# A hybrid of attention, convolution and expert layers: moving set-up work of the first stages beside the first attention, and the output's turn beside the last experts

## The chip, the cores and the metric

One core of a Trainium2 chip runs the whole program; the time is the device time of one execution in microseconds (us). Three runs of the kernel before gave a median of 1975.84 us (1970.2 to 1978.46).

## What is computed

The input is x, 4 images of 128 channels with 32 x 32 points, that is 4 batches of 1024 tokens. Six layers follow, each added to its input; the first two and the end are what matters here.

```python
x = x + _L0_conv_ref(_gn(x), Wq, Wk, Wv, bq, bk, bv)      # one-head attention over 1024 points per image
x = x + _L1_conv_ref(_gn(x), ...)                         # 3 scales: 3x3 depthwise convolutions, 8-head attention
...
t = t + _L3_ffn_ref(_ln_t(t), ...)                        # 8 dense gelu experts, weighted by a router
x = _from_tokens(t, x)                                    # tokens back to channels

def _gn(v, G=32, eps=1e-05):                              # group norm: 4 channels x 1024 points per group
    g = v.reshape(B_, G, C_ // G, H_, W_)
    m = jnp.mean(g, axis=(2, 3, 4), keepdims=True)
    s = jnp.var(g, axis=(2, 3, 4), keepdims=True)
    return ((g - m) / jnp.sqrt(s + eps)).reshape(v.shape)
```

## The kernel before

The program is a row of stages. Each stage is a `Block`: five instruction streams, one per engine (TensorE, VectorE, ScalarE, GpSimd and SyncE, which issues most of the transfers), that run by semaphores and meet at the block's end. A `Stage` hands its semaphores back when it ends, one clearing instruction each on GpSimd. Engines keep the order in which the code writes their instructions, so a wait in a stream holds back all that is behind it.

The stages that the change touches, in order:

- `make_identities` (L107): SyncE loads all of x (2 MB) in one transfer into `x_channels` (channels in the partitions, 4 x 1024 columns) and waits for it, while GpSimd makes two identity matrices.
- `group_norm` "gn0" (L130): VectorE takes `bn_stats` of 8 half batches, aggregates, a 128 x 8 matmul with `c_group` averages over the groups, ScalarE takes a root, VectorE a reciprocal; then VectorE normalises 4 batches, 1024 columns each, into `normalised_channels`.
- `one_head_attention` "attn0" (L243): SyncE loads six weights and waits for them, then runs `search.sync` (a search for edges that VectorE does beside batches 0 and 1; its first transfer is `edges_raw`) and `clear_routed`. GpSimd clears `zeros` (128 x 5200) and copies each batch into `attn_xs`. TensorE projects q, k, v; per batch it goes through 8 tiles of 128 queries: scores, turning of the exponentials, mixing with v, turning of the output, which VectorE adds into `x_channels` (`add_turned`, L439). TensorE and ScalarE run batches 0 to 2 as a loop.
- `scaled_attention_block` (L2919): a stage of its own loads 12 small `taps` (L2936) and clears three bordered images `padded` on GpSimd (L2943); then `group_norm` "gn1" does again for the new x what gn0 did, normalising into the middle of `padded`; then `conv_head_inputs` (L1141) loads 18 projection weights, makes diagonal matrices of the taps on ScalarE (`make_diagonals`, L1274) and works in 6 rounds (4 batches at full size, then two coarser scales). In a round TensorE convolves (9 taps, each a 128 x 128 diagonal times 512 columns, L1242) and projects; VectorE makes the position term with 8 multiply-adds (`position`, L1325) and splits q and k into three bf16 parts.
- `gelu_experts` "experts3" (L2482): 8 groups of 512 tokens, a loop over groups on TensorE and ScalarE; per expert TensorE does one 128 x 512 product (`experts_h_bank`, L2527) and four 128 x 128 ones (L2521), ScalarE the gelu, VectorE the weighted sum into `x_channels` (L2565).
- `turn_activations` "to_channels" (L502): TensorE turns 32 tiles of 128 tokens (L525), VectorE copies 8 groups of 512 columns back (L532), and SyncE stores a batch (512 KB) as soon as its two groups are there (L539).

Of the kernel before, what the change touches and what calls it, by code (L numbers as in the profile page):

```python
# [6 lines left out]
F32 = mybir.dt.float32  # L7
# [71 lines left out]
class Machine:  # L79


    def __init__(self, nc, ctx, ins):
# [10 lines left out]
        self.rounds = 0  # L93
        self.y_out = [nc.alloc_semaphore(f"y_out{i}") for i in range(STEP_TILES // 5)]
# [12 lines left out]
def make_identities(m):  # L107

    nc = m.nc
    with Stage(nc) as ctx:  # L110
        zeroed, made, loaded = (m.sem(f"i_{x}", ctx) for x in ("zeroed", "made", "loaded"))
# [18 lines left out]
def group_norm(m, name, out_of, eps=1e-5):  # L130

    nc = m.nc
    with Stage(nc) as ctx:
        sb = lambda n, s, dt=F32: m.sb(f"{name}_{n}", s, dt, ctx)
        group, stats, mv, moments = sb("group", [P, P]), sb("stats", [P, B * 2, 6]), sb("mv", [P, B, 2]), sb("moments", [P, 2, B])
        gm, rstd, tmp, epsb = sb("gm", [P, 2, B]), sb("rstd", [P, B]), sb("tmp", [P, B]), sb("eps", [P, 1])
        ps = m.psum(f"{name}_ps", [P, 2 * B], ctx)
        loaded, ready, summed, rooted, dve_step = (m.sem(f"{name}_{x}", ctx) for x in ("loaded", "ready", "summed", "rooted", "dve"))
        block = ctx.enter_context(nc.Block())

        @block.sync
        def _(sp):
            sp.dma_start(group[:], m.ins["c_group"]).then_inc(loaded, 16)

        @block.tensor
        def _(pe):
            pe.wait_ge(loaded, 16)
            pe.wait_ge(ready, 1)
            pe.matmul(ps[:], group[:], flat(moments[:]), start=True, stop=True).then_inc(summed, 1)

        @block.scalar
        def _(act):
            act.wait_ge(ready, 2)
            act.activation(tmp[:], rstd[:], ACT.Sqrt, bias=epsb[:]).then_inc(rooted, 1)

        @block.vector
        def _(dve):
            step = Chain(dve, dve_step)
            step(dve.memset(epsb[:], eps))
            for b in range(B):  # L160
                for h in range(2):
                    last = dve.bn_stats(stats[:, 2 * b + h, :], m.xc[:, b, h * 512:(h + 1) * 512])
# [2872 lines left out]
```

## Time and profile before

| what | value |
|---|---|
| median of 3 runs | 1975.84 us (1970.2 to 1978.46) |
| the profiled execution, first to last instruction or transfer | 1999.1 us |
| TensorE busy | 1666.4 us, 83% of the span |
| VectorE busy | 1334.0 us, 67% |
| ScalarE busy | 1004.8 us, 50% |
| GpSimd busy | 293.4 us, 15% |
| TensorE's mean granted clock | 0.910 of full speed |

The profile is that of one execution, which took 23.3 us (1.2%) longer than the median of the runs shown; its span is all that it lists of its time. Times in the rows below are microseconds from the span's start. Shares of the whole span say little here, since the stages have different limits: what a stage waits for is read from its own stretch of the timeline.

### The profile page before, as it was taken

The numbers are of one execution on the slowest core, as the hardware profiler recorded it, in microseconds if no ns is written. First come the engines' busy times: TensorE is split into PE (matmuls) and PEld (weight loads), VectorE is DVE, ScalarE is ACT, GpSimd is POOL, SyncE is SP. The second block draws the span as 40 slices with busy tenths as digits, with TensorE's granted clock in tenths as the row PEclk, the third lists the DMA queues.
The fourth block names the chain that finished last, engine by engine and source line by source line (L and its number), as shares of the span: only waits on it lengthen the run. The fifth ranks groups of instructions, "written<-read, shape, count | busy, mean of one in ns | idle before, by whom it ended". The sixth has DMA issues, their size and how long they took to land. (4 is left out here: it accounts for less than half of the span.)

```text
span 1999.1 us, 29912 instructions
## 1 busy us (share of the span) xinstructions
PE 1666.4 (83%) x9244; PEld 864.8 (43%) x9244; DVE 1334.0 (67%) x2664; ACT 1004.8 (50%) x1883; POOL 293.4 (15%) x300
## 2 busy tenths in 40 slices
PE   4999598799999998589776169945999999996998
PEld 2767344122222223475554158832222222225676
DVE  4753589888888866346766224446888888856566
ACT  2555233276766775014433146634377777675343
POOL 1010200101100011100023535550000110011000
PEclk9999799699999998699987579967699999997899
DMA  2260039024454410104000132137423223300001
GB/s 82 97 143 6 18 111 225 25 34 81 78 91 76 72 45 14 24 5 129 5 18 22 37 93 77 41 102 196 100 50 60 54 54 54 54 15 22 0 0 42
DMA packets 116627, 122.70 MB, mean 61 GB/s; under 512 B 24203, under 2 KB 90355, under 8 KB 115495
## 3 DMA queue, kind: packets, MB, share of 16 engines
q1 hardware_dynamic: 101118, 102.13, 22.6%
q0 software_dynamic: 15408, 19.31, 3.4%
q8 instruction: 52, 0.85, 0.2%
q14 instruction: 49, 0.40, 0.1%
HBM read 79.06 MB, written 41.84 MB: 60 GB/s over the span
## 5 line engine op out<-in xcount | busy, mean ns | idle before, releaser
L1037 DVE TENSOR_REDUCE heads_mx<-scales_n_bank 128x1 f32<-128x1024 f32 (+2 forms) x280 | 324.4, 1196 | 61.3 <-PE scales_n_bank L903 59.7
L1037 DVE TENSOR_REDUCE heads_mx<-edge_n_bank 128x1 f32<-128x1024 f32 x256 | 301.6, 1219 | 52.0 <-PE edge_n_bank L903 50.6
L1018 ACT ACTIVATE heads_prob<-scales_t_bank 128x512 f32<-128x512 f32 x512 | 264.5, 603 | 139.9 <-PE scales_t_bank L922 139.9
L1018 ACT ACTIVATE heads_prob<-edge_t_bank 128x512 f32<-128x512 f32 x512 | 264.5, 603 | 134.4 <-PE edge_t_bank L922 134.4
L903 PE MATMUL scales_n_bank<-scale_ks,scale_qs 96*128 96x512 bf16 (+2 forms) x608 | 177.4, 383 | 27.4 <-DVE heads_mx L1037 14.1
L903 PE MATMUL edge_n_bank<-edge_ks,edge_qs 99*128 99x512 bf16 x512 | 164.6, 406 | 24.5 <-PEq L43 13.5
L922 PE MATMUL scales_t_bank<-scale_qs,scale_ks 99*128 99x512 bf16 (+2 forms) x608 | 170.1, 368 | 3.5 <-ACT heads_prob L1018 3.5
L922 PE MATMUL edge_t_bank<-edge_qs,edge_ks 102*128 102x512 bf16 x512 | 155.5, 383 | 3.5 <-ACT heads_prob L1018 3.5
L938 PE MATMUL edge_o_bank<-heads_prob,edge_vs 128*32 128x512 f32 x1024 | 136.4, 605 | 0.1
L938 PE MATMUL scales_o_bank<-heads_prob,scale_vs 128*32 128x512 f32 x1024 | 136.4, 605 | 0.0
L903 PEld LDWEIGHTS scales_n_bank<-scale_ks,scale_qs 96*128 96x128 bf16 (+1 forms) x608 | 46.7, 101 | 176.2 <-issue 99.8
L2453 DVE TENSOR_TENSOR experts_hidT<-experts_gate,experts_hp_bank 128x256 f32<-128x256 f32 x80 | 33.6, 421 | 112.8 <-ACT experts_gate L2428 83.1
L903 PEld LDWEIGHTS edge_n_bank<-edge_ks,edge_qs 99*128 99x128 bf16 x512 | 39.5, 99 | 159.0 <-issue 89.7
L922 PEld LDWEIGHTS scales_t_bank<-scale_qs,scale_ks 99*128 99x128 bf16 (+1 forms) x608 | 57.9, 101 | 97.7 <-ACT heads_prob L1018 49.3
L2565 DVE SCALAR_TENSOR_TENSOR x_channels<-experts_o_bank,combine,x_channels 128x128 f32 (+1 forms) x256 | 72.1, 344 | 41.2 <-PE experts_o_bank L2521 40.1
L2393 PE MATMUL experts_hp_bank<-experts_xT,experts_w_now 128*128 128x128 f32 x640 | 92.0, 288 | 8.8 <-ACT experts_w_now L2433 5.9
L922 PEld LDWEIGHTS edge_t_bank<-edge_qs,edge_ks 102*128 102x128 bf16 x512 | 49.3, 98 | 99.3 <-ACT heads_prob L1018 54.4
L2370 POOL DMA_INDIRECT expert_y<-experts_ys,experts_aims x80 | 78.0, 975 | 81.4 <-DVE experts_ys L2464 74.3
L1983 POOL DMA_INDIRECT routed_x<-attn_rows,attn_slots x64 | 61.4, 960 | 192.7 <-DVE attn_slots L2286 174.4
L2393 PEld LDWEIGHTS experts_hp_bank<-experts_xT,experts_w_now 128*128 128x128 f32 x640 | 80.6, 197 | 19.4 <-issue 18.2
L1242 PE MATMUL in_c_bank<-padded,scale_diag 128*128 128x512 f32 (+1 forms) x198 | 83.7, 582 | 5.1 <-ACT scale_diag L1274 5.1
L2540 ACT ACTIVATE experts_hid<-experts_h_bank,gelu_b 128x512 f32<-128x512 f32 x64 | 44.0, 687 | 72.8 <-PE experts_h_bank L2527 72.8
(362 smaller groups left out, 2690.1 us busy)
## 6 DMA issues: line engine op xcount, KB each, us to landing
edges_text<-edges_targets SPq DMA_DIRECT2D x16, 512.0 KB, 3.6
scale_qs<-scale_q_parts SPq DMA_DIRECT2D x60, 128.0 KB, 4.9
scale_ks<-scale_k_parts SPq DMA_DIRECT2D x60, 128.0 KB, 6.9
heads_wide<-heads_inverse_d POOLq DMA_DIRECT2D x15, 512.0 KB, 9.6
edge_qs<-edge_q_parts SPq DMA_DIRECT2D x48, 128.0 KB
edge_ks<-edge_k_parts SPq DMA_DIRECT2D x48, 128.0 KB
routed_x<-attn_zeros SPq DMA_DIRECT2D x2, 2600.0 KB
experts_xs<-routed_x SPq DMA_DIRECT2D x16, 325.0 KB
```

The costliest lines, as they stand in the source:

```text
L903: last = pe.matmul(ps[0:TN, at_:at_ + CH], query(b, slice(0, KB), s, h, j, t * TN, TN), key(b, slice(0, KB), s, j, i * CH, CH), start=True ...
L922: last = pe.matmul(t_ps[i][0:TN, first:first + CH], key(of, slice(0, KM), c // NH, j, t * TN, TN), query(of, slice(0, KM), c // NH, c % NH ...
L938: last = pe.matmul(o_ps[SLOT * j:SLOT * (j + 1), 0:CH], vs[:, of if whole else 0, t, (4 * s + j) * SLOT:(4 * s + j + 1) * SLOT], prob[i][: ...
L1018: act.activation(to[:], t_ps[score_bank(of, place, g)[0]][0:TN, 0:HP * CH], ACT.Exp, scale=scale).then_inc(exped, 1)
L1037: dve.tensor_reduce(mx[:, u % UC:u % UC + G], scores, AX.X, ALU.max, negate=True).then_inc(first_used, 1)
L1242: last = pe.matmul(c_ps[:, c * CH:(c + 1) * CH], weights[i].diag[:, tap, :], chunk_window(r, tap, c), start=(tap == 0), stop=(tap == 8))
L1983: pool.indirect_dma_start(out=routed.x, out_offset=bass.IndirectOffsetOnAxis(ap=slots[f][:, i, t:t + 1], axis=0), in_=rows[:, f * T + t, i ...
L2370: pool.indirect_dma_start(out=routed.y, out_offset=bass.IndirectOffsetOnAxis(ap=aims[:, j:j + 1], axis=0), in_=ys[:, j, :], in_offset=None ...
L2393: last = pe.matmul(h_ps[j % 2][:, k * P:(k + 1) * P], w_now[j % 2][:, k * P:(k + 1) * P], xT[j % 2][:], start=True, stop=True)
L2453: dve.tensor_tensor(hidT[j % 2][:].rearrange("p k t -> p (k t)"), gate[j % 2][:].rearrange("p k t -> p (k t)"), h_ps[j % 2][:, hidden:2 * ...
L2540: act.activation(hid[e % 2][:], h_ps[e % 2][:], ACT.Gelu, bias=b1s[:, e:e + 1]).then_inc(made, 1)
L2565: last = dve.scalar_tensor_tensor(out=tile, in0=o_ps[e % 2][:, t * P:(t + 1) * P], scalar=weight, in1=tile, op0=ALU.mult, op1=ALU.add)
```

## The change

What it does, part by part. x is loaded in four transfers, one a batch, with the norm's matrix after the first; the attention's six weights follow; no engine waits for them in that block. Both group norms become a class whose pieces are called inside other blocks. The first norm's statistics, moments and root run at the head of the attention's block, VectorE normalises batch 0 straight into `attn_xs`, and GpSimd normalises batches 1 to 3 in place of its copies. The taps and projection weights (30 transfers) are issued by SyncE at the head of the attention's block, ahead of the search; GpSimd clears `padded` and makes the 27 diagonals there. The second norm's 8 `bn_stats` are spread over the attention's tiles on VectorE; the rest of that norm stands at the head of the convolution stage, where VectorE normalises batch 0 and GpSimd batches 1 to 3. The last experts' loop is written out on TensorE; in group g, after the products of expert 2, TensorE turns group g - 1, ScalarE copies it back behind the gelu of expert 4, and SyncE stores it (256 KB); `turn_activations`, with nothing left to do, goes. `token_norm` and the causal branches of the first attention, which nothing calls, go too.

```diff
-def make_identities(m):
+def begin_loads(m, norm, attention):
...
         @block.sync
         def _(sp):
-            sp.dma_start(m.xc[:], m.ins["x"].rearrange("b c h w -> c b (h w)")).then_inc(loaded, 16)
-            sp.wait_ge(loaded, 16)
+            for b in range(B):
+                sp.dma_start(m.xc[:, b, :], m.ins["x"][b].rearrange("c h w -> c (h w)")).then_inc(m.x_loaded[b], 16)
+                if b == 0:
+                    norm.load(sp)
+            attention.load(sp)
...
-def group_norm(m, name, out_of, eps=1e-5):
+class GroupNorm:
...
+    def note_spread(self, dve, b, h):
+        dve.bn_stats(self.stats[:, 2 * b + h, :], self.m.xc[:, b, h * 512:(h + 1) * 512]).then_inc(self.spread, 1)
+
+    def find(self, dve, ps):
+
+        step = Chain(dve, self.step)
+        step(dve.memset(self.epsb[:], self.eps))
+        dve.wait_ge(self.spread, 2 * B)
+        for b in range(B):
+            last = dve.bn_aggr(self.mv[:, b, :], self.stats[:, 2 * b:2 * b + 2, :])
+        step(last)
+        step(dve.tensor_tensor(self.tmp[:], self.mv[:, :, 0], self.mv[:, :, 0], ALU.mult))
+        step(dve.tensor_copy(self.moments[:, 0, :], self.mv[:, :, 0]))
+        dve.tensor_tensor(self.moments[:, 1, :], self.mv[:, :, 1], self.tmp[:], ALU.add).then_inc(self.ready, 1)
+        dve.wait_ge(self.summed, 1)
...
+        dve.reciprocal(self.rstd[:], self.tmp[:]).then_inc(self.found, 1)
+
+    def normalise(self, eng, b, dst, src):
+        eng.wait_ge(self.found, 1)
+        return eng.tensor_scalar(dst, src, self.gm[:, 0, b:b + 1], self.rstd[:, b:b + 1], ALU.subtract, ALU.mult)
...
-def one_head_attention(m, name, wq, wk, wv, bq, bk, bv, scale, causal, routed=None, search=None):
+def first_attention(m, name, weights, before, after, images, routed, search):
...
         def _(sp):
...
+            images.load(sp)
+            search.sync(sp)
+            clear_routed(sp, routed, zeros, zeroed, cleared)
 
         @block.gpsimd
         def _(pool):
...
+            search.prepare(pool)
+            aim_spare(pool, zeros, zeroed, cleared, 0)
+            images.prepare(pool)
             for b in range(1, B):
                 pool.wait_ge(S["v_made"], b)
-                pool.tensor_copy(xs[:], m.xnT[:, b, :]).then_inc(S["staged"], 1)
...
+                before.normalise(pool, b, xs[:], m.xc[:, b, :]).then_inc(S["staged"], 1)
...
         @block.vector
         def _(dve):
...
+            def measure_half(b, h):
+                dve.wait_ge(S["added"], b * T + 4 * h + 4)
+                after.note_spread(dve, b, h)
+
             for b in range(B):
...
+                dve.wait_ge(m.x_loaded[b], 16)
+                for h in range(2):
+                    before.note_spread(dve, b, h)
+            before.find(dve, r_ps[:, 0:2 * B])
+            before.normalise(dve, 0, xs[:], m.xc[:, 0, :]).then_inc(S["staged"], 1)
...
+                    if b >= 1 and t == 2:
+                        measure_half(b - 1, 1)
+                    if t == 6:
+                        measure_half(b, 0)
...
+            measure_half(B - 1, 1)
+            dve.wait_ge(after.spread, 2 * B)
+
+
+class Images:
...
+    def prepare(self, pool):
+        for one in self.padded:
+            pool.memset(one[:], 0.0).then_inc(self.bordered, 1)
+        pool.wait_ge(self.tap_loaded, 12 * 16)
+        for i in range(3):
+            for tap in range(9):
+                pool.tensor_scalar(self.weights[i].diag[:, tap, :], self.m.ident[:], self.taps[i][:, 0, tap:tap + 1], None, ALU.mult).then_inc(self.diag_made, 1)
...
-def conv_head_inputs(m, name, sizes, scratch, padded, taps, ins, first):
+def conv_head_inputs(m, name, sizes, scratch, images, norm, first):
...
         @block.sync
         def _(sp):
-            for one in weights:
-                one.load(sp)
...
                 pool.memset(v[:, p, :].rearrange("p (t d) -> p t d", d=SLOT)[:, :, HD:SLOT], 1.0).then_inc(ones, 1)
+            for b in range(1, B):
+                norm.normalise(pool, b, inside(b), raw(b)).then_inc(normed, 1)
...
-            make_diagonals(0)
             begin_position(0)
...
-                if r < 2:
-                    make_diagonals(r + 1)
...
+            norm.find(dve, v_ps[:, 0:2 * B])
+            norm.normalise(dve, 0, inside(0), raw(0)).then_inc(first_normed, 1)
             dve.wait_ge(ones, 2)
             position(0, *range(1, 9))
...
-def gelu_experts(m, name, n_experts, weights, combine, combineT, xn):
+def gelu_experts(m, name, n_experts, weights, combine, combineT, xn, out):
...
+        @block.sync
+        def _(sp):
+            for g in range(GROUPS):
+                b, h = divmod(g, GROUPS // B)
+                sp.wait_ge(taken, g + 1)
+                sp.dma_start(out[b].rearrange("c h w -> c (h w)")[:, h * 512:(h + 1) * 512], m.xc[:, b, h * 512:(h + 1) * 512]).then_inc(stored, 16)
+            sp.wait_ge(stored, GROUPS * 16)
...
+            def turn(g):
+                pe.wait_ge(added, 2 + (g + 1) * E)
+                if g >= 1:
+                    pe.wait_ge(taken, g)
+                for t in range(TG):
+                    last = pe.transpose(c_ps[:, t * P:(t + 1) * P], m.tt[:, g * TG + t, :], m.ident[:])
+                last.then_inc(turned, 1)
...
+                    if e == 3 and behind:
+                        turn(g - 1)
                 closing(E - 1)
+
+            for g in range(GROUPS):
+                group(g, g >= 1)
+            turn(GROUPS - 1)
...
+            def take(g):
+                act.wait_ge(turned, g + 1)
+                act.activation(flat_x[:, bass.ds(g * 512, 512)], c_ps[:], ACT.Copy).then_inc(taken, 1)
...
+                    if e == 4 and behind:
+                        take(g - 1)
...
-        turn_activations(m, "to_channels", out)
```

## Rows read from the trace of the kernel before

**Rows 1.** Windows of three stages: length, busy PE, PEld, DVE, ACT, POOL, clock, DMA share, GB/s:

```profile
211.00:232.00 21.00, 0.91 (x3) 0.84 (x4) 9.48 (x24) 2.38 (x5) 5.90 (x4) 0.58 0.05 5
232.00:370.00 138.00, 123.74 (x356) 57.63 (x355) 118.15 (x126) 44.51 (x67) 17.96 (x11) 0.91 0.50 136
1858.00:1990.00 132.00, 128.56 (x709) 91.63 (x707) 86.52 (x282) 54.26 (x72) 0.00 (x0) 0.97 0.00 0
```

**Rows 2.** Timeline of the start (start us, us, engine, line, operation; idle before, releaser):

```profile
0.75 0.44 SPq L116 DMA_DIRECT2D x_channels<-x  x1
...
8.89 4.84 DVE L162 BATCH_NORM_STATS2 gn_stats<-x_channels 128x6 f32<-128x512 f32 x8
...
14.43 0.17 DVE L168 COPY gn_moments<-gn_mv 128x4 f32<-128x4 f32 x1
...
16.68 2.98 DVE L178 TENSOR_SCALAR normalised_channels<-x_channels,gn_gm,gn_rstd 128x1024 f32<-128x1024 f32 x4
...
25.36 6.03 PE L316 MATMUL attn_s_bank<-attn_xs,attn_w 128*128 128x512 f32 x8 [9.85 <-DMA attn_bvb<-L_conv_bv]
```

**Rows 3.** DMA view of 0 to 12 us: the load of x:

```profile
x_channels<-x SPq DMA_DIRECT2D x1, 2048.0 KB, 7.6
```

**Rows 4.** Timeline between first attention and convolution stage:

```profile
210.60 0.29 DVE L439 TENSOR_TENSOR x_channels<-attn_r_bank,x_channels 128x128 f32<-128x128 f32 x1 [0.48 <-PE attn_r_bank L342]
...
213.83 5.44 POOL L2943 MEMSET padded<- 128x4624 f32 x3 [75.63 <-issue]
```

**Rows 5.** Timeline of the convolution stage's first round:

```profile
231.54 1.84 POOL L1228 MEMSET in_values<- 128x1024 f32 x2 [12.27 <-POOLq L43]
231.66 25.03 PE L1242 MATMUL in_c_bank<-padded,scale_diag 128*128 128x512 f32 x54 [5.12 <-ACT scale_diag L1274]
...
258.44 1.28 DVE L1333 SCALAR_TENSOR_TENSOR in_x<-in_p_bank,scale_bqk,in_pos 128x1024 f32<-128x1024 f32 x1 [8.55 <-PE in_p_bank L1253]
```

**Rows 6.** Timeline inside the first attention: VectorE in batch 0, TensorE for batch 1:

```profile
52.92 1.23 DVE L456 TENSOR_REDUCE attn_neg<-attn_s_bank 128x1 f32<-128x1024 f32 x1 [0.92 <-PE attn_s_bank L335]
...
69.69 1.88 PE L316 MATMUL attn_s_bank<-attn_xs,attn_w 128*128 128x512 f32 x4
```

**Rows 7.** Timeline of VectorE beside GpSimd around 1335 us:

```profile
1334.90 0.94 POOL L1453 MEMSET edge_values<- 128x1024 f32 x1
1334.90 1.03 DVE L1507 TENSOR_SCALAR in_wqk<-in_wqk 128x128 f32<-128x128 f32 x1
```

**Rows 8.** Costliest groups on GpSimd, shapes kept apart:

```profile
L976 POOL TENSOR_TENSOR heads_out<-heads_out,heads_wide 128x1024 f32 x6 | 14.1, 2354 | 50.6 <-DMA heads_wide<-heads_inverse_d 50.6
...
L1719 POOL MEMSET attn_zeros<- 128x5200 f32 x1 | 4.4, 4421 | 0.0
L2943 POOL MEMSET padded<- 128x4624 f32 x1 | 4.0, 3951 | 75.6 <-issue 75.6
...
L125 POOL TENSOR_SCALAR_AFFINE_SELECT ident<-ident 128x128 f32<-128x128 f32 x1 | 0.3, 283 | 0.2 <-POOL identb L122 0.2
```

**Rows 9.** Groups on ScalarE: activation table loads of the first attention:

```profile
L414 ACT ACT_TABLE_LOAD x3 | 3.8, 1283 | 0.1
```

**Rows 10.** Timeline of the last experts and of the output:

```profile
1983.61 1.02 PE L2527 MATMUL experts_h_bank<-normalised_channels,gelu_w 128*128 x2
...
1985.36 1.02 PE L2527 MATMUL experts_h_bank<-normalised_channels,gelu_w 128*128 x2
...
1987.32 2.35 DVE L2565 SCALAR_TENSOR_TENSOR x_channels<-experts_o_bank,combine,x_channels 128x128 f32<-128x128 f32 x8 [0.62 <-PE experts_o_bank L2521]
...
1989.99 3.86 PE L525 MATMUL to_channels_ps_bank<-ident,x_channels 128*128 128x128 f32 x32 [1.67 <-PEq L43]
1990.66 4.88 DVE L532 COPY x_channels<-to_channels_ps_bank 128x512 f32<-128x512 f32 x8 [0.99 <-PE to_channels_ps_bank L525]
1991.97 3.92 SPq L539 DMA_DIRECT2D out<-x_channels  x4
```

**Rows 11.** Window at the very end (columns as in rows 1):

```profile
1997.00:1998.00 1.00, 0.00 (x0) 0.00 (x0) 0.00 (x0) 0.00 (x0) 0.00 (x0) 0.50 0.99 401
```

More of the change, by code:

```diff
@@ L243, in one_head_attention @@
-def one_head_attention(m, name, wq, wk, wv, bq, bk, bv, scale, causal, routed=None, search=None):
+        self.m, self.eps = m, eps
+        self.group = group if group is not None else sb("group", [P, P])
+        self.stats, self.mv, self.moments = sb("stats", [P, B * 2, 6]), sb("mv", [P, B, 2]), sb("moments", [P, 2, B])
+        self.gm, self.rstd, self.tmp, self.epsb = sb("gm", [P, 2, B]), sb("rstd", [P, B]), sb("tmp", [P, B]), sb("eps", [P, 1])
+        self.loaded, self.spread, self.ready, self.summed, self.rooted, self.found, self.step = (
+            m.nc.alloc_semaphore(f"{name}_{x}") for x in ("loaded", "spread", "ready", "summed", "rooted", "found", "dve"))
@@ new lines, in load, with tensor, scalar @@
+    def load(self, sp):
+        sp.dma_start(self.group[:], self.m.ins["c_group"]).then_inc(self.loaded, 16)
+    def note_spread(self, dve, b, h):
+        dve.bn_stats(self.stats[:, 2 * b + h, :], self.m.xc[:, b, h * 512:(h + 1) * 512]).then_inc(self.spread, 1)
+    def tensor(self, pe, ps):
+        pe.wait_ge(self.ready, 1)
+        pe.matmul(ps, self.group[:], flat(self.moments[:]), start=True, stop=True).then_inc(self.summed, 1)
+    def scalar(self, act):
+        act.wait_ge(self.ready, 2)
+        act.activation(self.tmp[:], self.rstd[:], ACT.Sqrt, bias=self.epsb[:]).then_inc(self.rooted, 1)
@@ L306, in _ @@
         def _(pe):
-            pe.wait_ge(S["loaded"], 16 * (4 if causal else 6))
+            pe.wait_ge(before.loaded, 16)
+            before.tensor(pe, r_ps[:, 0:2 * B])
+            pe.wait_ge(weights.loaded, weights.LOADS)
             def project(b, i):
@@ L383, in _ @@
         def _(act):
-            act.wait_ge(S["loaded"], 16 * (4 if causal else 6))
+            before.scalar(act)
+            act.wait_ge(weights.biased, weights.BIASES)
             def scale_out(b, t):
@@ L1149, in conv_head_inputs @@
         sb = lambda nm, s, dt=F32: m.sb(f"{name}_{nm}", s, dt, ctx)
-        weights = [ScaleWeights(m, ctx, i, ins) for i in range(3)]
+        weights, padded, taps, diag_made = images.weights, images.padded, images.taps, images.diag_made
+        inside = lambda b: padded[0][:, b, 1:H + 1, 1:W + 1]
+        raw = lambda b: m.xc[:, b, :].rearrange("p (y x) -> p y x", x=W)
         ROOM = max(FULL, B * (sizes[1] + 2) * sizes[1])
@@ L1233, in _ @@
         def _(pe):
+            norm.tensor(pe, v_ps[:, 0:2 * B])
             def convolve(r, c):
@@ L1271, in _ @@
         def _(act):
-            def make_diagonals(i):
-                for tap in range(9):
-                    act.activation(weights[i].diag[:, tap, :], m.ident[:], ACT.Copy, scale=taps[i][:, 0, tap:tap + 1]).then_inc(diag_made, 1)
+            norm.scalar(act)
             def begin_position(r):
```

368 lines of the change are left out of this document (106 added, 262 removed).

## The prediction

> **What bounds the kernel now.** The chain of waits on the page covers only the last 9 us, so I read by stage. First the windows: they part the stretches in which TensorE is full from those in which nothing is. Between the first attention and the convolutions lie 21.0 us in which TensorE is busy for 0.91 us, at a granted clock of 0.58, while in the last experts it is busy for 128.56 of 132 us [rows 1]. So work taken out of that gap shortens the program, and work put on TensorE in the last experts lengthens it. Then the timeline of three places, each read for what TensorE waits for. At the start its first projection stands at 25.36 us, behind the load of x, the norm and six weights, of which it names the last, after 9.85 us idle [rows 2]. At the boundary the attention's last addition begins at 210.60 and the first convolution at 231.66 [rows 4, 5]: taps, clearing, norm and diagonals stand in a row there. At the end the last weighted sum is done at 1987.32 + 2.35 = 1989.67 us and the span ends at 1999.1; turning, copying and storing lie between [rows 10]. These three places are the change's subject. In the attention and in the convolutions' first round VectorE itself waits for TensorE (0.92 us before a maximum, 8.55 us before the first q) [rows 5, 6], so there is room for small work beside them.
>
> **Part A, the start.** SyncE issues eleven transfers where it issued one and waited. An issue takes 0.44 us [rows 2], so the block ends at 0.75 + 11 x 0.44 = 5.6 us. The hand-over to the next stage took 0.54 us (x landed 7.6 us after 0.75, the statistics began at 8.89) [rows 2, 3], so they begin at 6.2 and take the same 4.84 us: 11.0. All of x lands about when it did, 8.35, and batch 3 is wanted at 6.2 + 6 x 0.605 = 9.8, so no statistic waits for it. The small copy of the moments came 0.70 us after the statistics' end (13.73 to 14.43), and 2.25 us later the normalisation began (16.68) [rows 2]. Here the change brings GpSimd in: from about 6.2 it clears `zeros` (4.42 us), with its small instructions to 11.1, then the first `padded` image (3.95 us) to 15.1 [rows 8]. A copy and a tensor-scalar operation of VectorE beside such clearing cost extra: at 1334.90 a 128 x 128 tensor-scalar took 1.03 us, as long as the GpSimd memset that began with it (0.94 us), while eight times the columns took 2.98 / 4 = 0.75 us where GpSimd was idle [rows 2, 7]. It got through only when the memset was over. No row shows the 128 x 4 copy in that place. Its bounds are no wait at all and the whole rest of the memset, 15.1 - 11.7 = 3.4 us; I take the wait, since the row at 1334.90 is the nearest. Then 2.25 us to the normalisation, up to 0.3 us for one diagonal of GpSimd in its way (0.28 us for the nearest one-input operation of that size) [rows 8], and 0.75 us for one batch in place of four: 18.4, and the projection at 18.5 against 25.36. **Gain 6.9 us**; 9.4 if only the big normalisation waits, to 15.1; 4.2 if the issues are held back so that the stage begins at 8.9 as before.
>
> The Trainium skill states the rule in "SBUF — State Buffer", section "SBUF: two separate sides": VectorE and GpSimd share one pair of ports, whichever starts first holds it for its whole instruction, and the other is fully blocked; "Advanced Engine Details and Errata", section "VectorE Performance Modes", counts copies with source and target in SBUF and even sizes among the operations that need the pair. The trace agrees for the tensor-scalar (1.03 us beside 0.94). By that rule the copy waits too, and the sum is the one taken here; it speaks against this placing.
>
> What else moves past SyncE's queue there: 30 loads ahead of the search, 30 x 0.44 = 13.2 us, so `edges_raw` is issued at 19.4. VectorE wants it after v, 8 us behind the projection, at 26 or later: no cost. GpSimd's normalisation for batch 1 (between 0.94 us, a memset of 1024 columns, and 2.35 us, a two-input operation) [rows 7, 8] may get in the way of the search's packing: 0 to 2.3 us, taken as nothing, since GpSimd's copy stood there before. The later ones have 44 us each (25.36 to the next projection at 69.69) [rows 2, 6]. The eight statistics of the second norm cost 0.61 us each inside tiles where VectorE waits 0.92 us [rows 6]: nothing, until that cover is thinner than 0.61 us.
>
> **Part B, the boundary.** VectorE ends its last addition at 210.89 and adds one statistic, 211.5; hand-over 0.54; the norm without its eight statistics took 16.68 - 13.73 = 2.95 us [rows 2, 4]: batch 0 may be normalised at 215.0. GpSimd restarts 2.9 us after the attention's end (213.83 against 210.89), having cleared the semaphores, and now begins with two memsets of values, 1.84 us [rows 4, 5]: 214.4 to 216.3. The normalisation waits that out and ends at 217.05; the first convolution stands at 217.2 against 231.66. **Gain 14.5 us**; 15.8 without the wait; 12.1 if GpSimd's own normalisation of batch 1 (up to 2.35 us) is served first. TensorE's 54 convolution matmuls, 25.03 us, then decide when q of round 0 is there [rows 5], so TensorE's gain counts, and VectorE's position work, held up by three GpSimd normalisations (at most 7.1 us), is hidden by its 8.55 us of idle time, which grows as VectorE starts no later than TensorE gains. The diagonals leave ScalarE; it was busy for 44.51 of 138 us [rows 1]: nothing. TensorE stands idle before this start as it did, so no change of its clock is counted.
>
> **Part C, the end.** Four turns per group are added to TensorE, which is full: 3.86 / 32 = 0.12 us each, 0.48 us a group [rows 10], seven groups, **3.4 us lost**. ScalarE's copy fits: an expert takes 1985.36 - 1983.61 = 1.75 us. In return the tail shrinks. It is 9.4 us now. After: 0.15 us to start, 0.48 turning, 0.2, one copy of 0.61 us (4.88 / 8) [rows 10], 0.1 to the issue. From the first issue at 1991.97 to the end are 7.1 us, of which 2.1 MB at 401 GB/s are 5.2 [rows 10, 11]; with 0.26 MB it is 1.9 + 0.65 = 2.55. Sum 4.1, **gain 5.3**; net 1.9, between 0.5 and 2.5.
>
> **Sum.** 6.9 + 14.5 + 1.9 = 23.3 us off a profiled span of 1999.1. That execution was 23.3 us longer than the median of the runs shown, which I take as spread over all stages, so the same gain is taken off the median: 1975.84 - 23.3 = 1952.5 us.
>
> **Rivals.** (1) The small copy slips past GpSimd's clearing. Against it is the blocked tensor-scalar [rows 7], for it that this copy has 4 columns: 2.5 us more gained, 1950.0. (2) The lower bounds come together (issues held back, GpSimd first at the boundary, dear turns): 4.2 + 12.1 + 0.5 = 16.8, 1959.0. (3) ScalarE's copy among the gelus calls for a table load of 1.28 us before and after it: 2.56 us less the 0.4 us free between two gelus, seven times, 15.1 us lost: 1967.6. Against it: the attention's loop mixes exponentials and copies and has three loads for three rounds of the loop [rows 9]. (4) **Slower than before:** the 27 diagonals on GpSimd. They start at about 16.6 us and stand ahead of batch 1's normalisation, which TensorE wants at 18.5 + 44.3 = 62.8; so they may cost (62.8 - 2.35 - 16.6) / 27 = 1.62 us each. Beyond, each further us costs 27: from 2.5 us the whole gain is gone, at 3 us the time is 1990. For it: this form, with its factor read from a column, is in no row; against it the nearest, 0.28 us [rows 8]. (5) The change does not do what it says: what is saved at the boundary comes back as a wait of the rounds after it, since VectorE is busy for 118.15 of 138 us there [rows 1]. It would leave less than 9.9 us. Against it: the 8.55 us of idle time in round 0 are all that VectorE could lose.
>
> **How the numbers follow.** A measurement of this kernel tells 0.5% or 9.9 us from no change. Forecast 0.47, (1) 0.24, (2) 0.14: faster, 0.85. (3) 0.06 and (5) 0.05: same, 0.11. (4): slower, 0.04. The bounds of the unknown costs give gains of 16.8 to 27.7 us, 1948.1 to 1959.0; the runs shown lie up to 5.6 us below and 2.6 above their median, which makes it 1944 to 1963, with (3), (4) and (5) left out.
>
> **What would show it.** In the changed profile: the first projection at about 18.5 us with the 128 x 4 copy of the moments drawn out to over 3 us beside a memset; no table load between gelu and copy; first convolution some 6.3 us after the attention's last addition; the groups of the last experts 0.4 to 0.5 us longer; one 256 KB store after the last sum. Wrong would be: diagonals over 1.6 us each, a maximum of VectorE that no longer waits for TensorE in the tiles with a statistic, or TensorE waiting for `edges_raw` or the staged batch 1.

## The result, and the profile after

The changed kernel took 1946.41 us (median of four runs, 1943.94 to 1948.81) against 1973.26 of the kernel before (four runs): ratio 0.9865, 95% interval 0.9848 to 0.9882. Two more sets of five and six runs on other occasions gave 0.9882 (0.9857 to 0.9906) and 0.9892 (0.9870 to 0.9913). The forecast, 1952.5 us with a gain of 23.3, is a ratio of 0.988. The measured 1946.41 is 6.1 us below the forecast and inside its range. The profiled execution of the changed kernel spans 1942.1 us, its own time is 1943.94.

The start, from its timeline (start us, us, engine, line, operation, tiles; in brackets idle time and releaser), to be held against [rows 2, 8]:

```profile
7.63 4.84 DVE L150 BATCH_NORM_STATS2 gn_stats<-x_channels 128x6 f32<-128x512 f32 x8 [7.63 <-PEq L43]
...
12.57 5.46 POOL L439 MEMSET padded<- 128x4624 f32 x3
...
13.24 4.43 DVE L169 COPY gn_moments<-gn_mv 128x4 f32<-128x4 f32 x1
...
18.04 16.79 POOL L443 TENSOR_SCALAR scale_diag<-ident,taps 128x128 f32<-128x128 f32 x27
...
19.78 0.92 DVE L180 TENSOR_SCALAR attn_xs<-x_channels,gn_gm,gn_rstd 128x1024 f32<-128x1024 f32 x1
...
20.85 5.65 PE L258 MATMUL attn_s_bank<-attn_xs,attn_w 128*128 128x512 f32 x8 [2.27 <-DVE attn_xs L180]
...
34.82 3.78 POOL L180 TENSOR_SCALAR attn_xs<-x_channels,gn_gm,gn_rstd 128x1024 f32<-128x1024 f32 x1
```

The statistics begin at 7.63 us, not 6.2. The copy of the moments, 0.17 us alone, took 4.43 us beside GpSimd's clearing, and the projection follows at 20.85 where it stood at 25.36. The diagonals on GpSimd cost 16.79 / 27 = 0.62 us each, and GpSimd's normalisation of a batch 3.78 us.

The boundary, from the timeline, against [rows 4, 5]:

```profile
205.07 0.29 DVE L370 TENSOR_TENSOR x_channels<-attn_r_bank,x_channels 128x128 f32<-128x128 f32 x1 [0.48 <-PE attn_r_bank L282]
...
208.59 1.84 POOL L1141 MEMSET in_values<- 128x1024 f32 x2 [73.38 <-issue]
...
209.41 1.57 DVE L180 TENSOR_SCALAR padded<-x_channels,gn_gm,gn_rstd 128x1024 f32<-128x1024 f32 x1
...
210.41 13.00 POOL L180 TENSOR_SCALAR padded<-x_channels,gn_gm,gn_rstd 128x1024 f32<-128x1024 f32 x3
...
211.03 25.89 PE L1161 MATMUL in_c_bank<-padded,scale_diag 128*128 128x512 f32 x54 [2.80 <-DVE padded L180]
...
238.67 1.28 DVE L1249 SCALAR_TENSOR_TENSOR in_x<-in_p_bank,scale_bqk,in_pos 128x1024 f32<-128x1024 f32 x1 [9.98 <-PE in_p_bank L1172]
```

First convolution 211.03 - 205.07 = 5.96 us after the last addition began; it was 231.66 - 210.60 = 21.06. So 15.1 us are gained. But the 54 convolution rows (matrix products of 512 columns) take 25.89 us where they took 25.03, and the first q (VectorE's first sum of a projection and the position term, at 238.67) comes 27.64 us behind the first of them where it came 26.78 us behind (258.44 - 231.66). The windows show why (columns as in [rows 1]); first the changed kernel, then the kernel before:

```profile
211.00:217.00 6.00, 5.97 (x8) 2.54 (x9) 4.56 (x3) 2.48 (x2) 6.00 (x2) 0.59 0.00 0
```

```profile
232.00:238.00 6.00, 6.00 (x11) 2.49 (x11) 2.74 (x3) 4.21 (x9) 5.94 (x4) 0.76 0.34 83
```

In the six us in which the convolutions begin the clock was granted at 0.59, in the kernel before at 0.76. It has two levels, listed as 0.50 and 1.00 (1.2 and 2.4 GHz), so these means are about 4.9 and 2.9 us at the half level. Counted from the first convolution that is 4.9 us here and 3.2 there: 1.7 us more at half the pace, worth the 0.9 us.

The end, from the timeline, against [rows 10]:

```profile
1804.76 2.04 PE L2453 MATMUL experts_b_bank<-gelu_b,experts_share 8*128 8x128 f32 x8 [1.74 <-DVE experts_share L2505]
...
1808.89 1.28 ACT L2490 ACT_TABLE_LOAD   x1 [11.23 <-PE experts_h_bank L2466]
...
1823.78 1.15 PE L2453 MATMUL experts_b_bank<-gelu_b,experts_share 8*128 8x128 f32 x8
...
1839.85 1.15 PE L2453 MATMUL experts_b_bank<-gelu_b,experts_share 8*128 8x128 f32 x8
...
1935.31 2.36 DVE L2522 SCALAR_TENSOR_TENSOR x_channels<-experts_o_bank,combine,x_channels 128x128 f32<-128x128 f32 x8 [0.63 <-PE experts_o_bank L2460]
```

The same bias products in the kernel before:

```profile
1860.58 2.06 PE L2514 MATMUL experts_b_bank<-gelu_b,experts_share 8*128 8x128 f32 x8 [1.77 <-DVE experts_share L2548]
...
1878.84 1.15 PE L2514 MATMUL experts_b_bank<-gelu_b,experts_share 8*128 8x128 f32 x8
...
1894.47 1.15 PE L2514 MATMUL experts_b_bank<-gelu_b,experts_share 8*128 8x128 f32 x8
```

A bias product opens each group of 512 tokens, so the time from one to the next is what a group takes. From the first bias product to the end of the last weighted sum are 1937.67 - 1804.76 = 132.91 us, 129.09 before (from 1860.58). From there to the end of the span are 4.4 us, 9.4 before. A group with a turn (the four 128 x 128 products that bring the group before it back to channels) takes 16.07 us, the first one, without a turn, 19.02; in the kernel before they took 15.63 and 18.26. No table load stands between the gelus and ScalarE's copies; the only one of the stage is that of 1808.89, behind the first h product.

The two profiled spans differ by 57.0 us, twice what the runs say. The profiled execution of the kernel before lost 26 us between the fusion (the stage that joins the three scales) and the second experts, in code that is the same in both kernels; the first experiment shows it with a second trace of the kernel before, and the stages are compared with that one below.

### The profile page after: what moved, and what is told of

It is laid out like the page before. It is cut to its first block and busy times, and to the rows that moved or that the text cites. A ratio compares the mean times of both kernels' runs of the same rounds, so it can differ in the third digit from the quotient of the medians.

```text
span 1942.1 us, 29755 instructions
## 1 busy us (share of the span) xinstructions
PE 1654.9 (85%) x9244; PEld 857.4 (44%) x9244; DVE 1331.3 (69%) x2650; ACT 991.6 (51%) x1857; POOL 331.6 (17%) x329
## 3 DMA queue, kind: packets, MB, share of 16 engines
q1 hardware_dynamic: 101598, 102.07, 23.3%
## 5 line engine op out<-in xcount | busy, mean ns | idle before, releaser
L2314 PEld LDWEIGHTS experts_hp_bank<-experts_xT,experts_w_now 128*128 128x128 f32 x640 | 80.0, 196 | 16.1 <-issue 14.5
```

What stands on the lines that cost most here:

```text
L2314: last = pe.matmul(h_ps[j % 2][:, k * P:(k + 1) * P], w_now[j % 2][:, k * P:(k + 1) * P], xT[j % 2][:], start=True, stop=True)
```

## The experiments

Five experiments have one run each (the two-input copy, the late statistics, the work in the pause, the diagonals, the gelu ahead). They are read by their own stage and not by their whole times, which lie between 1946.11 and 1966.16 us.

**The kernel before, once more, and the changed kernel, once more.** No edit.

> The kernel before unaltered, for a second trace. Theory: the traced execution of before was drawn out by 20 us or more in code that the change does not touch (its span of 1999.1 lies above all its timed runs); then this span is 1968 to 1977, first convolution at 231.7 and last experts of 129.1 us as before, and against the changed kernel the difference from the fusion to the second experts falls from 26 us to 10 or less. Rival: the change itself makes those stages faster (other timing of its loads); then the difference of 26 us between the fusion and the second experts stays.

Span 1973.8 us. Timelines of the second trace: first projection, first convolution (the row is cut off by the window that was asked for), fusion, second experts, last experts:

```profile
25.66 5.18 PE L316 MATMUL attn_s_bank<-attn_xs,attn_w 128*128 128x512 f32 x8 [9.85 <-DMA attn_bvb<-L_conv_bv]
...
230.59 9.83 PE L1242 MATMUL in_c_bank<-padded,scale_diag 128*128 128x512 f32 x19 [5.12 <-ACT scale_diag L1274]
...
833.47 2.05 PE L2822 MATMUL fuse_f_bank<-fuse_w,scale_out 128*128 128x128 f32 x8 [13.75 <-PEq L43]
...
1143.74 0.69 PE L2385 MATMUL experts_xp_bank<-ident,experts_xs 128*128 128x128 f32 x2 [29.37 <-DMA experts_xs<-routed_x]
...
1835.36 2.07 PE L2514 MATMUL experts_b_bank<-gelu_b,experts_share 8*128 8x128 f32 x8 [1.78 <-DVE experts_share L2548]
```

The same two rows of the first trace:

```profile
828.45 2.04 PE L2822 MATMUL fuse_f_bank<-fuse_w,scale_out 128*128 128x128 f32 x8 [13.24 <-PEq L43]
...
1164.33 0.69 PE L2385 MATMUL experts_xp_bank<-ident,experts_xs 128*128 128x128 f32 x2 [29.29 <-DMA experts_xs<-routed_x]
```

From the fusion to the second experts: 335.9 us in the first trace, 310.3 in the second, 309.6 in the changed kernel. So the 26 us belonged to that one execution. They lie inside the attention `attn2`, where two rows of `attn_x_bank` stand 170.2 us apart in the first trace (955.64 and 1125.79) and 144.1 in the second (960.99 and 1105.09); what drew it out is open. Boundary and last experts are as in the first trace (21.06 us at the boundary, 129.05 us of last experts, 9.4 of tail).

> The changed kernel unaltered, as the base for the runs below. By the traces the changed places give 4.5 (first projection) + 1.0 (attention) + 15.1 (boundary) - 0.9 (first convolutions) + 1.1 (last experts and tail) = 20.8 us, the medians gave 26.9. If those traced parts are all there is, the ratio comes nearer to 1 - 20.8/1973 = 0.9895; if something downstream in unchanged code gets faster as well, it stays at about 0.9865, a gain near 27 us.

Ratio 0.9882 (0.9857 to 0.9906): between the two readings, and the interval holds both. The start of its timeline:

```profile
12.08 5.47 POOL L439 MEMSET padded<- 128x4624 f32 x3
...
12.74 3.32 DVE L169 COPY gn_moments<-gn_mv 128x4 f32<-128x4 f32 x1
...
19.20 5.39 PE L258 MATMUL attn_s_bank<-attn_xs,attn_w 128*128 128x512 f32 x8 [2.23 <-DVE attn_xs L180]
```

Here the copy ended at 16.06 us, just behind the end of the first clearing (12.08 + 3.96); in the changed kernel's first trace it ended at 17.67, behind the second one. Of the eight traces with the copy in that place, five have 3.3 us and three 4.4. Second trace against second trace the gain is 25.66 - 19.20 = 6.5 us at the start, 15.1 at the boundary, -0.9 in the first convolutions, -3.85 in the last experts and +5.0 in the tail: 21.8. The spans differ by 20.7 (1973.8 and 1953.1); the stages that were not touched make up the rest, and they differ by as much as 8 us between two executions of one kernel: from the first q to the fusion 567.4 and 575.5 us in the changed one, 570.0 and 576.3 in the kernel before. These two pairs also show no loss of the boundary's gain in the rounds behind it.

**GpSimd's clearing and diagonals later.**

```
             aim_spare(pool, zeros, zeroed, cleared, 0)
+            pool.wait_ge(S["staged"], 1)
             images.prepare(pool)
```

> GpSimd clears the padded images and makes the diagonals only once VectorE has normalised batch 0. Theory (the copy of the moments was held by the clearing): the 128 x 4 copy takes 0.17 us in place of 4.43, the normalisation starts at 15.5 instead of 19.78, the first projection at 16.6 instead of 20.85, and all later stages move by 4.3 us: about 1942. GpSimd's 27 diagonals then end near 38 us and are still hidden. Rival: the copy waits for something else (its own queue, a semaphore), and still ends at 17.7; or the projection waits for a weight or a bias instead and the gain is under 1 us.

```profile
12.74 0.17 DVE L169 COPY gn_moments<-gn_mv 128x4 f32<-128x4 f32 x1
...
14.99 0.81 DVE L180 TENSOR_SCALAR attn_xs<-x_channels,gn_gm,gn_rstd 128x1024 f32<-128x1024 f32 x1
...
15.95 5.17 PE L259 MATMUL attn_s_bank<-attn_xs,attn_w 128*128 128x512 f32 x8 [2.13 <-DVE attn_xs L180]
```

As the theory has it: the copy takes 0.17 us, and the projection stands at 15.95. The first q comes at 232.95, 3.6 us ahead of the changed kernel's second trace. The ratio of the runs, 0.9880 (0.9856 to 0.9904), can't resolve 3.6 us.

**The copy as a two-input operation.**

```
-        step(dve.tensor_copy(self.moments[:, 0, :], self.mv[:, :, 0]))
+        step(dve.tensor_tensor(self.moments[:, 0, :], self.mv[:, :, 0], self.mv[:, :, 0], ALU.max))
```

> The copy of the moments (one input) becomes a maximum of the same four columns with themselves (two inputs), all else as in the changed kernel. Theory (only some forms of VectorE need what GpSimd's clearing holds; the two-input multiplication just ahead took its 0.16 us beside it): the instruction takes 0.17 us in place of 3.32 to 4.43, and the next one-input form, the normalisation of batch 0, comes at about 15.0 us and now waits itself until a clearing ends, at 16.0 or 17.1; projection at 17.0 to 18.2 against 19.2 to 20.9 in the changed kernel and 15.95 with the clearing moved. Rival (any VectorE instruction at this place waits, as the queue or the memory is what is busy): 3.3 us or more as before, projection at 19.2 or later.

```profile
12.18 5.99 POOL L439 MEMSET padded<- 128x4624 f32 x3
...
12.84 0.17 DVE L169 TENSOR_TENSOR gn_moments<-gn_mv 128x4 f32<-128x4 f32 x1
...
15.09 1.58 DVE L180 TENSOR_SCALAR attn_xs<-x_channels,gn_gm,gn_rstd 128x1024 f32<-128x1024 f32 x1
...
16.82 5.34 PE L258 MATMUL attn_s_bank<-attn_xs,attn_w 128*128 128x512 f32 x8 [2.90 <-DVE attn_xs L180]
```

The two-input form ran beside the clearing in 0.17 us; the wait moved to the normalisation, 1.58 us where it takes 0.81 with GpSimd idle. Projection at 16.82, a little earlier than expected. So it is the form of the instruction that waits, not the queue. The Trainium skill's "SBUF — State Buffer", section "SBUF: two separate sides", says so: the forms of VectorE that need the pair of ports which it shares with GpSimd hold it for a whole instruction, or are fully blocked while GpSimd holds it. The copies agree, ending with a clearing. The normalisation agrees less well: it ended 0.53 us after the first clearing (12.18 + 3.96), less than its 0.81; why is open.

**The second norm's statistics behind the attention.** The eight calls leave the attention's loop and stand ahead of the norm in the next stage.

```
-                    if b >= 1 and t == 2:
-                        measure_half(b - 1, 1)
-                    if t == 6:
-                        measure_half(b, 0)
...
+            for b in range(B):
+                for h in range(2):
+                    norm.note_spread(dve, b, h)
             norm.find(dve, v_ps[:, 0:2 * B])
```

> The eight statistics of the second norm go back behind the attention, in one row at the head of the next stage. Theory (hidden in the attention, 4.84 us on the path at the boundary): the first convolution stands 9.0 us after the last addition begun (5.7 to 6.0 in the changed kernel, plus 4.84, less the one statistic of 0.69 that stood there, less 0.8 because GpSimd's clearing of the values is then over when batch 0 is normalised), and the attention from its first projection to its last addition takes the same 184 us. Rival (the statistics cost something in the attention): that stretch gets shorter by 1 us or more, and the net cost is under 2.5 us.

```profile
205.86 0.29 DVE L370 TENSOR_TENSOR x_channels<-attn_r_bank,x_channels 128x128 f32<-128x128 f32 x1 [0.49 <-PE attn_r_bank L282]
...
215.36 26.29 PE L1156 MATMUL in_c_bank<-padded,scale_diag 128*128 128x512 f32 x54 [2.04 <-DVE padded L180]
```

The first convolution stands 9.50 us behind the last addition begun, half a us more than expected, and the attention takes 205.86 - 20.61 = 185.3 us where the changed kernel's traces have 183.9 to 184.2: it got no shorter. So the statistics cost nothing inside the attention, and 3.5 us behind it. The single run took 1966.16 us, more than this explains; part of the rest is again the stretch from the first q to the fusion, 579.4 us.

**Work for TensorE in the pause.**

```
+            pe.matmul(c_ps[:, 0:512], m.ident[:], m.xc[:, 0, 0:512], start=True, stop=True)
             norm.tensor(pe, v_ps[:, 0:2 * B])
+            pe.matmul(c_ps[:, 0:512], m.ident[:], m.xc[:, 0, 0:512], start=True, stop=True)
```

> Two products of 128 x 512, whose result is overwritten, are put on TensorE in the pause between attention and convolutions, one ahead of and one behind the norm's small product. The 54 convolution rows of the first batch took 25.0 us in the kernel before and 25.9 in the changed one, whose granted clock stood at 0.59 over the first six us. Theory (the pause lowers the clock, work in it keeps it): those rows take 23.2 to 24.5 us, the first q comes 25.0 to 26.5 us after the first convolution in place of 27.5. Rival (the clock falls whatever is done in the pause, or fell earlier): 25.9 and 27.5 as now, or the first convolution is late by up to 1.7 us behind the added products.

```profile
210.38 23.45 PE L1163 MATMUL in_c_bank<-padded,scale_diag 128*128 128x512 f32 x54 [1.84 <-DVE padded L180]
...
235.58 1.28 DVE L1251 SCALAR_TENSOR_TENSOR in_x<-in_p_bank,scale_bqk,in_pos 128x1024 f32<-128x1024 f32 x1 [7.54 <-PE in_p_bank L1174]
```

```profile
205.00:211.00 6.00, 3.06 (x8) 1.20 (x9) 3.66 (x14) 2.22 (x3) 3.06 (x3) 1.00 0.00 0
...
211.00:217.00 6.00, 6.00 (x16) 2.63 (x15) 5.17 (x4) 1.84 (x2) 6.00 (x2) 1.00 0.00 0
```

The clock stays at 1.00, the rows take 23.45 us, the first q comes 25.20 us behind the first convolution. So the 0.9 us were the clock, and 1.6 us were lost to it in the kernel before too (26.78 us). The loss is not a constant: of the eight traces that have the changed kernel's pause and no added work in it, seven took 25.75 to 26.30 us for these rows, and one (the next experiment) 25.07. The Trainium skill's "TensorE: Matmul & The Clock Gate", Part 1, calls the half rate the default that activity lifts; this run agrees, with 1.00 granted throughout beside the added work.

**The diagonals three times.** The two loops over images and taps run three times (81 instructions).

> GpSimd makes the 27 diagonals three times, 81 instructions. It tests how much cover they have. Theory (they stand ahead of batch 1's normalisation, which TensorE wants about 44 us after its first projection, at 63 to 65 us): from about 17.8 us, 81 x 0.61 = 49.6 us, done at 67.4, normalisation of 3.78 us done at 71.2, second projection at 71.3 and so 6 to 8 us late, the whole program as much longer. Rival (GpSimd's time does not matter there, or the cover is larger than reckoned): second projection at 63 to 65 us as now.

```profile
17.74 48.08 POOL L446 TENSOR_SCALAR scale_diag<-ident,taps 128x128 f32<-128x128 f32 x81
...
69.72 2.97 PE L258 MATMUL attn_s_bank<-attn_xs,attn_w 128*128 128x512 f32 x4 [3.86 <-POOL attn_xs L180]
```

They took 0.59 us each. TensorE now waits 3.86 us for GpSimd's normalisation, and the first four rows after that wait take 2.97 us where they took 1.88. The second projection stands 49.2 us behind the first where it stood 44.3 behind (65.10 - 20.85): 4.9 us late, less than the 6 to 8 expected for it. From first projection to first convolution are 196.9 us where they were 190.2, so the whole is 6.7 us late, as the theory said. The cover is real and holds about 1.5 us an instruction ((63.1 - 3.8 - 17.55) / 27, by the second trace of the changed kernel); 0.62 is well inside.

**A group turned one group later.**

```
+                    if e == 1 and g >= 2:
+                        turn(g - 2)
                     if e >= 1:
                         closing(e - 1)
-                    if e == 3 and behind:
+                    if e == 3 and g == GROUPS - 1:
                         turn(g - 1)
```

ScalarE's copies back move in step.

> Each group is turned one group later, at the place where TensorE waits 0.75 us for the first gelu of a group (its weight load's wait), so six of seven turns lie there and one stays where it is. From the first bias product to the last sum the changed kernel takes 132.9 us, the kernel before 129.1. Theory (TensorE stands idle there): 129.6 to 130.3, 2.5 to 3.3 us off the whole, about 1943.5. Rival (the wait of the weight load overlaps products that still run, TensorE has no gap): 132.5 to 133.5, no change.

```profile
1910.07 1.99 PE L2466 MATMUL experts_h_bank<-normalised_channels,gelu_w 128*128 128x512 f32 x4
...
1911.89 0.60 PE L2445 MATMUL experts_c_bank<-ident,x_channels 128*128 128x128 f32 x4
```

From the first bias product to the last sum are 131.8 us (1810.80 to 1942.61), between the two theories and nearer to the rival: 1.1 us won, which the ratio of the runs, 0.9879 (0.9855 to 0.9903), can't resolve. A group of this kernel without a turn takes 15.63 us, with the turn in the gap 15.88, with the turn further back, as in the changed kernel, 16.07. So 0.25 of the 0.44 us is still paid: the turn begins (1911.89) before the products ahead of it end (1910.07 + 1.99), so most of the 0.75 us that the weight load waits is no gap.

**One gelu ahead.** The three periods raised a question: the kernel before also takes 15.63 us for a group, so the turns explain 7 x 0.44 = 3.1 of the 3.85 us lost, and 0.76 lie in the first group (19.02 us, 18.26 before), which turns nothing.

```
             act.wait_ge(loaded, 64)
+            act.activation(spare[:], b1s[:, 0:1], ACT.Gelu)
```

> ScalarE applies one gelu to a single column, into a spare tile, before it waits for the first h product of the last experts. In the changed kernel the first group takes 19.02 us from bias product to bias product, in the kernel before 18.26, although neither turns anything in it; the later ones take 16.07 and 15.63. Theory (since its first group stands outside the loop, the load of the gelu table, 1.28 us, comes behind the wait for the first h product, where the kernel before had it ahead of that wait): the load stands ahead of the first bias product, the first group takes 18.2 to 18.4 us, bias product to last sum 132.1 to 132.3 in place of 132.9. Rival (TensorE's program, written out for eight groups where the kernel before has a loop, is what costs there): the first group still takes 19.0 us.

```profile
1811.09 1.28 ACT L2481 ACT_TABLE_LOAD   x1 [6.36 <-PEq L43]
...
1811.83 2.04 PE L2454 MATMUL experts_b_bank<-gelu_b,experts_share 8*128 8x128 f32 x8 [1.73 <-DVE experts_share L2507]
...
1830.02 1.15 PE L2454 MATMUL experts_b_bank<-gelu_b,experts_share 8*128 8x128 f32 x8
```

```profile
1859.96 1.28 ACT L2540 ACT_TABLE_LOAD   x1 [6.52 <-PEq L43]
```

The second fence is the kernel before, whose loop has the load at the head of every group, eight in all; the changed kernel has one. In this run the load is ahead of the bias product again, as in the kernel before, and the first group takes 18.19 us; bias product to last sum 132.1. The table load it was. That it lost its place because the first group was taken out of the loop follows from the two traces; no run took that step back by itself.

**The moves together, with and without added work.** The first is the clearing moved, the turn one group later, and the clearing of the values behind the first normalisation of the boundary (VectorE waits for it only ahead of the first values). What it adds to the edits above:

```
         def _(pool):
+            pool.wait_ge(first_normed, 1)
             for p in range(2):
```

The second has these moves too, and adds the products of the pause and four at the start:

```
+            def warm():
+                pe.matmul(s_ps[0][:, 0:512], m.ident[:], m.xc[:, 0, 0:512], start=True, stop=True)
+
+            pe.wait_ge(m.x_loaded[0], 16)
+            for i in range(3):
+                warm()
             pe.wait_ge(before.loaded, 16)
             before.tensor(pe, r_ps[:, 0:2 * B])
+            warm()
```

The third is the changed kernel unaltered, run beside them.

> The changed kernel with three moves and no added work: GpSimd's clearing and diagonals behind batch 0's first normalisation, its clearing of the values behind batch 0's second normalisation, and the turn of a group one group later. By the traces of the single moves: 3.3 us at the first projection (15.95 against 19.2), 0.8 at the first convolution (5.2 us after the last addition begun in place of 5.96), 1.1 in the last experts: 5.2 us off the changed kernel's 1948.6, about 1943, ratio to the kernel before 0.9855. Rival (the rounds of the convolutions or the search take back what the start gives): first q no earlier than 3 us ahead of the changed kernel's, and a ratio as the changed kernel's.

> The three moves, and added products whose results are overwritten: two in the pause ahead of the convolutions, and four ahead of the first projection (three before the first norm's small product, one behind it). By the pause's own run 2.3 us at the first q. At the start the same theory (work in the pause brings the clock up) makes the eight rows of the first projection take 3.6 us in place of 5.2 and the first score about 1.7 us earlier: in all 5.2 + 2.3 + 1.7 = 9.2 us off the changed kernel, about 1939.4, ratio 0.9835. Rival (four products at the start are too little to bring the clock up): the projection takes 5.2 us as now, and 7.5 us come off, 1941.

> The changed kernel unaltered, beside the two above. By the second trace of the kernel before against that of the changed kernel the gain is 20.7 us of span (1973.8 to 1953.1); the ratio should lie at 0.987 to 0.9895, the two above below it. The first projection falls at 19.2 to 19.4 where the copy of the moments gets in behind GpSimd's first clearing, at 20.6 to 20.9 where it waits for the second.

Ratios 0.9835 (0.9813 to 0.9856), 0.9842 (0.9822 to 0.9862) and, for the changed kernel beside them, 0.9892 (0.9870 to 0.9913): the moves alone beat both kernels, at 1941.87 us against 1953.72 and 1974.41. That is more than the 5.2 us expected. The traces give less: the first q comes 2.55 us earlier (234.21 against 236.76), under the 3 us that the rival named, though the ratio didn't come out as the rival's; with the last experts it is 3.7, and the rest lies within the spread of the untouched stages. The added products won nothing beyond the moves in the runs (1943.24 us), where 2.3 to 4.0 more were expected, though they did bring the first q to 232.55. The boundary of the two, the moves alone first:

```profile
205.35 0.81 DVE L180 TENSOR_SCALAR padded<-x_channels,gn_gm,gn_rstd 128x1024 f32<-128x1024 f32 x1
...
206.22 26.24 PE L1163 MATMUL in_c_bank<-padded,scale_diag 128*128 128x512 f32 x54 [2.04 <-DVE padded L180]
...
207.34 23.45 PE L1172 MATMUL in_c_bank<-padded,scale_diag 128*128 128x512 f32 x54 [0.19 <-DVE padded L180]
```

With the clearing of the values moved, VectorE's normalisation takes 0.81 us in place of 1.57, and the first convolution stands 5.21 us behind the last addition begun in place of 5.96: the wait at the boundary was that clearing. Without added work the rows take 26.24 us against 25.85 in the run beside it, so that of the 0.74 us gained at the first convolution 0.4 are left at the first q; since unaltered pauses gave 25.07 to 26.30, it is not shown that the earlier start cost this. With added work the rows take 23.45.

At the start the added products brought nothing that the traces can tell. The first projection's rows took 5.08 us, in the traces without added work 5.17 to 6.62, and first projection to last addition took 185.3 us, against 184.7 with the moves alone. The clock fell to the half level in the idle 1.18 us ahead of that projection; why it fell so soon is open.

```profile
12.00:18.00 6.00, 3.81 (x8) 1.36 (x7) 3.03 (x15) 0.30 (x1) 2.45 (x3) 0.82 0.26 50
```

In the run with the moves alone the windows list 1.00 over the same stretch, but its eight rows took 5.85 us, and at the pace of the convolutions' 23.45 / 54 = 0.43 us they would have taken 3.5. So the clock listed at the very start of the program doesn't fit the rows there.

## Why the prediction came out as it did

**Sum.** 23.3 us forecast; 21.8 by the places of the second traces, 21 to 27 by the three ratios. Every part lies within the bounds that the prediction gave it, for the reasons that it gave; three small terms were missed. That the total agrees within 2 us is in part luck: 0.4 us too much in A, 0.6 too little and 0.9 overlooked in B and 0.75 too much in C partly cancel, and stages that nobody touched vary by more. Two steps of the working don't hold. The bounds and the spread give 1948.1 - 5.6 = 1942.5 and 1959.0 + 2.6 = 1961.6, not 1944 and 1963; the measured 1946.41 lies in either range. And the 23.3 us by which the profiled execution was too long were not spread over all stages: 26 us of it lay in one attention, which the sum did not use.

**Part A** (6.9): 6.5 in the second traces, 4.5 in the first. The wait of the copy was predicted and is shown (clearing moved, form changed). Two sizes were off: the issues were held back (up to 1.03 us where the step put 0.44), so that the statistics began at 6.9 to 7.6, not 6.2, and what held them back is open; and the step let the copy in behind the first image, while in three of eight traces it came in behind the second. Without the wait the projection stands at 15.95.

**Part B** (14.5): 15.1. The wait for GpSimd's clearing of the values was there (1.57 us, alone 0.81) and is shown (clearing of the values moved). It was shorter than put: the clearing ended 5.36 us behind the last addition begun, not 5.7, and the normalisation 0.55 us behind the clearing, not 0.75. "No change of its clock is counted" is the step that failed: with the pause cut from 21 to 6 us the half level lasted 4.9 us into the convolutions in place of 3.2, and 0.9 us were lost; with the clock kept up the stretch is 2.4 us shorter. GpSimd's normalisation costs 3.78 to 4.3 us, not at most 2.35: the bound was taken from a two-input row, and this form is dearer. It was harmless, as VectorE idles 9.98 us before the first q. The statistics inside the attention were hidden, as forecast.

**Part C** (1.9): the turns cost 3.1 where 3.4 were forecast, the tail gave 5.0 where 5.3 were. Missed was the gelu table: with ScalarE's first group taken out of the loop its load lost its cover, 0.76 us. Net 5.0 - 3.85 = 1.15, inside the bounds.

**Rivals.** (1) did not happen: the copy never slipped past. (2) did not come together. (3) looked for table loads around the copy, where there are none; the one that cost something was at the head of the stage. (4) 0.62 us an instruction; the limit is about 1.5 us, not 1.62, since GpSimd's normalisation is dearer and the diagonals begin later. (5) did not happen in the rounds; what came back, 0.9 us in the first one, came by the clock and not by VectorE.

## What to carry to other kernels

Work moved beside other work is paid for where it shares something: ask what form each instruction has, and keep a long clearing on GpSimd away from the short one-input steps of a chain that everything waits for. When a pause is cut short, look at the granted clock behind it; when a loop's first pass is taken out of it, look where its table load went. One profiled execution can be 26 us off in code nobody touched: compare stage by stage, and take the other kernel's profile twice before explaining a difference.

## What the runs showed that was not expected

A GpSimd tensor-scalar with factors from columns took 3.78 us for 128 x 1024, where VectorE takes 0.81, but 0.6 us for 128 x 128. Beside it VectorE's two-input position steps stretched only from 10.53 / 8 = 1.32 us to 12.16 / 8 = 1.52, and GpSimd's from 3.78 to 4.3: neither was shut out, unlike the copy. In the run with work in the pause alone, both added products ran at full speed (1.10 us each) and the clock stood at 1.00; in the kernel with all moves and added work they took 1.79 and 2.00 us, and yet the convolutions behind them took the same 23.45. Its windows tell why: the clock did fall there, while the products ran, and was back when the convolutions began at 207.34.

```profile
204.00:207.00 3.00, 3.00 (x6) 1.05 (x4) 1.55 (x8) 0.83 (x2) 0.00 (x0) 0.51 0.00 0
207.00:213.00 6.00, 5.81 (x14) 2.56 (x14) 4.62 (x4) 1.24 (x1) 5.65 (x3) 1.00 0.00 0
```

So the gain of 2.4 us came twice, but that the added work keeps the clock up all through the pause is so in one of the two traces. And a table load came onto the path, for 0.76 us, when a loop's first pass was written out.
